# The last FFN with half of its tokens sorted by expert, and their routing done inside the Mamba stage

## The chip, the cores and the metric

The kernel runs on one core of one Trainium2 chip. The metric is device time in microseconds (us). TensorE (PE) multiplies matrices, and its weight loads (PEld) run beside it; VectorE (DVE), ScalarE (ACT) and GpSimd (POOL) do elementwise work; SyncE (SP) issues DMAs. Each engine takes its instructions strictly in the order in which they are written, and the engines wait for each other by semaphores.

## The reference

2048 tokens of 128 channels pass through six stages; the last three are `L1_ffn`, a Mamba layer, and `L1_ffn` again. `L1_ffn` is a mixture of experts with a shared part:

```
xf = layernorm(x).reshape(-1, 128)                       # 2048 tokens
shared = silu(xf @ shared_w1.T) * (xf @ shared_w2.T) @ shared_w3.T      # hidden 512
scores = sigmoid(xf @ router_w.T)                        # 8 experts
_, top_idx = top_k(scores + expert_bias, 2)
gates  = scores * one_hot(top_idx).sum(-2)               # zero for 6 of 8 experts
h1, h2 = split(einsum('td,ehd->teh', xf, w12))           # every token with every expert
routed = einsum('teh,edh->td', silu(h1) * h2 * gates, w3)
x = x + 0.5 * (shared + routed)
```

Only two of the eight experts of a token have a gate that isn't zero.

## The kernel before

The 16 tiles of 128 tokens lie in SBUF for the whole program. An FFN stage takes them in four blocks of 512 tokens (`BLK`), and each block as 12 **units** of 128 hidden channels: 4 shared ones and 8 experts. A unit is two projections (`up`, into the PSUM banks `ps_a` and `ps_b`), Silu on ACT (`gate`), a product on DVE (`gated`), for an expert a product with its gates, broadcast over the partitions, on POOL (`weigh`, L697), a split into a high and a low part on ACT and DVE (`high` L393, `low` L509), and one projection back (`down`, into `ps_acc`). Every projection is three matmuls of 512 columns (`three_pass`, L98 to L100: high times high, low times high, high times low). Experts are dense: each of the 8 is computed for all 512 tokens of a block, and gates of zero cancel 6 of them.

Routing of a block: three matmuls with the router, Tanh, top-8 and indices on DVE (`choose`), gates on POOL (`weights`), a transpose, a store of the gates to DRAM (`gate_rows`) and one broadcast load for each expert (`gate_row`, SP queue, `rows`).

The order is written out by hand. `up` leads by 4 units, `high` and `low` by 2, and every engine runs the same `body(n)`. The stages stand in blocks of their own with a barrier between them. `mamba_phase` runs eight sections (one for each sequence), each of four pieces q = 0 to 3 with `products`, `decay` and `outputs`; four of the sections stand in a hardware loop of two turns, and they also prepare the first two blocks of the following FFN (`turn_head`, `high_head`, `normal_head`: layernorm, transpose, split). The rest of the last sequence (`tail.*`: `to_tokens`, `turn_y`, `project_out`) lies in the beginning of the last FFN. In the first stage the SP queue also loads the weights of all later stages, between the gate rows (`loads`; `load_rest` at L2532 issues after the rows of block 1).

## Time and profile before

| | before |
|---|---|
| median of 3 runs (lowest to highest) | 723.2 us (720.96 to 723.59) |
| profiled execution: its own time | 724.5 us |
| profiled execution: span from first to last instruction | 722.5 us |
| mean granted TensorE clock | 0.987 |
| PE / DVE / ACT / POOL busy | 94% / 79% / 58% / 45% |
| Mamba ends, last FFN begins, last matmul of it begins | 603.35, 604.61, 717.35 us |

A busy PE isn't a PE at its peak: matmuls overlap by their modelled ends, so the distance between two starts, not the duration, is what one costs. The distance of starts within one kind of matmul is read off the timeline.

### The profile page before, as it was taken

The page shows a single profiled execution, that of the slowest core. Times are in us where ns is not written, and L with a number is a line of the kernel's source. Part 1 is how long each engine was busy: PE and PEld are TensorE (multiplying, and loading weights), DVE is VectorE, ACT ScalarE, POOL GpSimd, SP SyncE. Part 2 cuts the span into 40 slices and gives each one's busy share as a digit, 9 for nine tenths or more (in the row PEclk, how much of TensorE's full clock was granted, in tenths as well). Part 3 has the DMA queues.
Part 4 walks back from the last instruction along what each step waited for, and adds up shares of the span by engine and source line. Part 5 has one row for each costly group of instructions (what it writes and reads, how often), then busy time and mean ns, then how long its engine had stood idle before and what let it go on. Part 6 is the DMA issues. An engine that isn't in the chain of part 4 may idle for free. (4 is left out here: it accounts for less than half of the span.)

```text
span 722.5 us, 12386 instructions
## 1 busy us (share of the span) xinstructions
PE 677.4 (94%) x4100; PEld 506.3 (70%) x4100; DVE 569.2 (79%) x1308; ACT 419.3 (58%) x757; POOL 324.5 (45%) x404
## 2 busy tenths in 40 slices
PE   7899998797899999999999878999999998999997
PEld 5667774643457777777778676777777775777785
DVE  5789978989978888988989855666766676879774
ACT  4557686885245555556656647555565555455553
POOL 2568884101227766465658461220413200555463
PEclk9999999999999999999999989999999999999999
DMA  6625430000013232222213100000000000323131
GB/s 168 200 89 187 137 110 1 0 1 0 1 52 125 70 108 90 88 59 81 96 59 90 29 1 1 2 2 2 1 2 0 0 1 2 117 74 118 56 122 44
DMA packets 34329, 43.16 MB, mean 60 GB/s; under 512 B 5216, under 2 KB 17504, under 8 KB 34272
## 3 DMA queue, kind: packets, MB, share of 16 engines
q1 hardware_dynamic: 34272, 42.46, 19.1%
q8 instruction: 29, 0.48, 0.3%
q14 instruction: 28, 0.23, 0.1%
HBM read 41.13 MB, written 1.31 MB: 59 GB/s over the span
## 5 line engine op out<-in xcount | busy, mean ns | idle before, releaser
L697 POOL TENSOR_TENSOR p_prod<-p_p,p_gate_row 128x512 f32<-128x512 f32 x128 | 203.5, 1602 | 108.7 <-DVE p_p L504 62.4
L384 ACT ACTIVATE p_sil<-p_ps_a 128x512 f32<-128x512 f32 x176 | 105.3, 598 | 131.1 <-PE p_ps_a L100 126.8
L509 DVE TENSOR_TENSOR p_hlo<-p_prod,p_hhi 128x512 fp32r<-128x512 f32 x176 | 149.6, 851 | 0.3 <-ACT p_hhi L393 0.2
L504 DVE TENSOR_TENSOR p_p<-p_sil,p_ps_b 128x512 f32<-128x512 f32 x128 | 87.1, 681 | 54.3 <-ACT p_sil L384 37.3
L393 ACT CAST p_hhi<-p_prod 128x512 fp32r<-128x512 f32 x176 | 108.1, 615 | 24.9 <-POOL p_prod L697 24.9
L98 PE MATMUL p_ps_a<-xt_hi,w_uphi 128*128 128x512 f32 x176 | 74.2, 422 | 0.0
L98 PE MATMUL p_ps_acc<-p_hhi,w_downhi 128*128 128x512 f32 x176 | 71.1, 404 | 1.2 <-DVE p_hlo L509 1.0
L98 PE MATMUL p_ps_b<-xt_hi,w_uphi 128*128 128x512 f32 x176 | 71.2, 404 | 0.1
L100 PE MATMUL p_ps_a<-xt_hi,w_uplo 128*128 128x512 f32 x176 | 70.1, 398 | 0.0
L99 PE MATMUL p_ps_a<-xt_lo,w_uphi 128*128 128x512 f32 x176 | 70.1, 398 | 0.0
L100 PE MATMUL p_ps_b<-xt_hi,w_uplo 128*128 128x512 f32 x176 | 69.8, 396 | 0.0
L99 PE MATMUL p_ps_acc<-p_hlo,w_downhi 128*128 128x512 f32 x176 | 69.5, 395 | 0.0
L99 PE MATMUL p_ps_b<-xt_lo,w_uphi 128*128 128x512 f32 x176 | 69.5, 395 | 0.0
L100 PE MATMUL p_ps_acc<-p_hhi,w_downlo 128*128 128x512 f32 x176 | 69.3, 394 | 0.0
L2185 DVE TENSOR_TENSOR mb_sm<-mb_sm,mb_c 128x512 f32<-128x512 f32 x64 | 43.8, 688 | 27.1 <-ACT mb_off L2069 21.1
L1910 PE MATMUL mb_c<-mb_bc 64*128 64x128 f32 (+1 forms) x512 | 58.9, 349 | 1.4 <-ACT mb_bc L2047 1.4
L2047 ACT COPY mb_bc<-mb_c 128x1024 f32<-128x1024 f32 x32 | 32.3, 1012 | 43.8 <-PE mb_c L100 43.8
L1910 PEld LDWEIGHTS mb_c<-mb_bc 64*128 64x128 f32 x512 | 38.9, 186 | 20.9 <-issue 16.0
L2192 DVE SCALAR_TENSOR_TENSOR mb_sm<-mb_d,mb_later 128x512 f32<-128x512 f32 x64 | 41.1, 684 | 15.0 <-PE mb_d L1885 14.8
L2066 ACT ACTIVATE mb_sm<-mb_sm 128x512 f32<-128x512 f32 x64 | 40.5, 632 | 16.9 <-DVE mb_sm L2192 15.9
L2332 POOL TENSOR_TENSOR w_downhi<-mb_widehi,mb_own 128x512 fp32r<-128x512 f32 x8 | 8.3, 1041 | 84.6 <-DVE norm_moments L2211 46.8
L98 PEld LDWEIGHTS p_ps_b<-xt_hi,w_uphi 128*128 128x128 f32 x176 | 33.3, 189 | 11.8 <-DVE p_p L504 2.8
(355 smaller groups left out, 1432.1 us busy)
## 6 DMA issues: line engine op xcount, KB each, us to landing
p_gate_row<-gate_rows SPq DMA_DIRECT2D x128, 256.0 KB, 3.3
w_rawbuf<-in_L_ffn_fc_w_dram SPq DMA_DIRECT2D x3, 512.0 KB, 7.0
w_rawbuf<-in_L_ffn_w_dram SPq DMA_DIRECT2D x3, 512.0 KB, 6.5
out_dram<-x SPq DMA_DIRECT2D x4, 256.0 KB, 3.5
w_rawbuf<-in_L_ffn_shared_w_dram SPq DMA_DIRECT2D x3, 256.0 KB, 5.8
x<-in_L_attn_x_dram SPq DMA_DIRECT2D x2, 256.0 KB, 3.9
x<-in_L_attn_x_dram SPq DMA_DIRECT2D x1, 512.0 KB, 9.2
mb_xraw<-in_L_attn_W_B_dram SPq DMA_DIRECT2D x1, 512.0 KB, 5.0
```

The lines of the kernel that those rows point to most:

```text
L98: pe.matmul(out, weights[0], moving[0], start=start, stop=False)
L99: pe.matmul(out, weights[0], moving[1], start=False, stop=False)
L100: return pe.matmul(out, weights[1], moving[0], start=False, stop=stop)
L384: nc.scalar.activation(sil[:, u % 2], ps_a[:, u % 2], ACT.Silu).then_inc(c["sil"].sem, 1)
L393: nc.scalar.copy(hhi[:, u % R], prod[:, u % R]).then_inc(c["hhi"].sem, 1)
L504: nc.vector.tensor_tensor(dst, sil[:, u % 2], ps_b[:, u % 2], ALU.mult).then_inc(c["p1"].sem, 1)
L509: nc.vector.tensor_tensor(hlo[:, u % R], prod[:, u % R], hhi[:, u % R].bitcast(F32), ALU.subtract).then_inc(c["hlo"].sem, 1)
L697: G.tensor_tensor(prod[:, u % R], p1[:, u % 2], gate_row[:, e % ROWS], ALU.mult).then_inc(c["prod"].sem, 1)
L1910: last = pe.matmul(half(q, t, more)[:, k, 0:SEQ - t * P], bc[h][state, r, j, bass.ts(t, P)], bc[h][state, 2 + r, j, t * P:SEQ], start=True ...
L2066: A(sm[q % 2][t][:], sm[q % 2][t][:], ACT.Exp).then_inc(c["m_E"].sem, 1)
L2185: V.tensor_tensor(sm[q % 2][t][:], sm[q % 2][t][:], half(q, t, more)[:, :, 0:P], ALU.mult).then_inc(c["m_read"].sem, 1)
L2192: V.scalar_tensor_tensor(out=sm[q % 2][t][:], in0=ps_d[t][:], scalar=0.0, in1=later[:].unsqueeze(1).broadcast_to([P, 4, P]), op0=ALU.min, ...
```

## The change

Blocks 0 and 1 of the last FFN (8 tiles, 1024 tokens) keep their 4 shared units; their experts are computed on sorted tokens. Blocks 2 and 3 stay as they are.

- **In Mamba.** The layernormed rows of blocks 0 and 1 stay in `xraw`. `TokenSort.logits` (12 small matmuls for each block), `bend` (Tanh) and `choose` route them in the two loop sections with a `head`; in the last section `rank` (9 matmuls with triangular matrices) and `places` (nine small DVE operations) work out, for each token and each of its two experts, a row of a sorted list in which each expert begins at a multiple of 128. POOL then scatters rows by indirect DMA into `sorted_rows` in DRAM: 4 tiles, two DMAs each, at the end of Mamba, 4 more at the beginning of the FFN. The hardware loops are written out. `outputs(h, m, 0)` stands ahead of `to_tokens` there, and PE waits for the Tanh (`gth`) or for `z_slot` in between, since the logits and ranks lie in `to_tokens`' bank.
- **In the last FFN** (`sparse_stream`, new). `SLOT_TILES` = 23 tiles of 128 sorted rows in six groups (5 of 4, one of 3) follow the four shared units of block 0. PE reads the expert of each tile into a register (`z_owners`, 23 loads spread over units 0 to 3); each tile is transposed, multiplied with the weights of its own expert with the tokens as the stationary side (`three_pass_turned`: 3 matmuls of 256 columns up, 3 of 128 down), stored to DRAM, and gathered by 16 indirect DMAs on POOL. ACT multiplies with the gates (`z_weigh`), POOL adds (`z_add`). The gates of block 2 are applied by DVE, those of block 3 by POOL; there are 8 buffers for gate rows, not 4.
- **In the first stage.** `load_rest` first fills `sorted_rows` with zeros (23 tiles, 1.5 MB).

```diff
+def three_pass_turned(pe, out, tokens, weights):
+    pe.matmul(out, tokens[0], weights[0], start=True, stop=False)
+    pe.matmul(out, tokens[0], weights[1], start=False, stop=False)
+    return pe.matmul(out, tokens[1], weights[0], start=False, stop=True)
...
+    def logits(self, pe, b, xt, router, bank):
+        pe.wait_ge(c["xlo"].sem, c["xlo"].at(b + 1))
+        for j in range(BT):
+            some = bass.ts(b * BT + j, P)
+            last = three_pass(pe, self.logits_of(bank)[:, j], [q[:, some] for q in xt], [q[:] for q in router], True, True)
+        last.then_inc(c["z_lg"].sem, 1)
...
+    def scatter(self, j):
+        for k in range(2):
+            self.nc.gpsimd.indirect_dma_start(self.rows_dram[:, :], bass.IndirectOffsetOnAxis(ap=self.place[:, k, j:j + 1], axis=0),
+                                              self.xn[:, j], None).then_inc(self.c["z_scat"].sem, 16)
...
+            def z_owners(g):
+                for q in range(g * SLOT_TILES // CUT, (g + 1) * SLOT_TILES // CUT):
+                    owner[q] = pe.value_load(sort.owner[0:1, q:q + 1], min_val=0, max_val=(EXPERTS - 1) * P)
...
+            def z_up(s):
+                pe.wait_ge(c["z_xlo"].sem, c["z_xlo"].at(s + 1))
+                for t in range(sizes(s)):
+                    some = bass.ds(owner[s * BT + t] * 2 + S * 2 * P, 2 * P)
+                    last = three_pass_turned(pe, raised(s)[:, t].rearrange("p a c -> p (a c)"),
+                                             [q[s % 2][:, bass.ts(t, P)] for q in (z_xhi, z_xlo)], [q[:, some] for q in up_flat])
...
+            for g in range(CUT):
+                step(g)
+            z_turn_x(1)
+            for s in range(GROUPS):
+                z_up(s)
+                if s:
+                    z_turn_h(s - 1)
+                if s >= 2:
+                    z_down(s - 2)
+                if s + 2 < GROUPS:
+                    z_turn_x(s + 2)
+                if s + 2 == GROUPS:
+                    turn_gates(2)
+            step(CUT)
+            z_turn_h(GROUPS - 1)
+            z_down(GROUPS - 2)
+            step(CUT + 1)
+            z_down(GROUPS - 1)
...
+            scale(2)
+            for j in range(SCATTERED, HALF):
+                sort.scatter(j)
+            scale(3)
+            weights(2)
+            for h in range(2):
+                kept = c[f"z_kept{h}"]
+                pool.wait_ge(kept.sem, kept.at(16 * (GROUPS // 2)))
+            for j in range(HALF):
+                sort.gather(j, z_back)
+                if j == 4:
+                    weights(3)
+            for b in range(2):
+                z_add(b)
...
-            with pe.Fori(0, 2) as i:
+            for i in range(2):
                 section(1, i * 2 + 3)
                 section(0, i * 2 + 4, head=i)
...
         def load_rest(sp):
 
+            sp.dma_start(rows_dram.rearrange("(t p) c -> p t c", p=P), kept["xraw"][:, 0:1].broadcast_to(
+                [P, SLOT_TILES, P])).then_inc(counts["z_blank"].sem, 16)
             w1_set.load(sp, slice(4, None))
             rw_set.load(sp, slice(0, None))
```

**SP in the first stage, between the gate rows of block 1 and of block 2.** Before:

```order
L786 DMA p_gate_row<-gate_rows 128x512 [waits s_prod] x7
L71 DMA w_rawbuf<-in_L_ffn_w_dram 128x4x256
L71 DMA w_rawbuf<-in_L_ffn_w_dram 128x8x128
L71 DMA rw_tm<-in_L_attn_W_tm_dram 128x384
L71 DMA rw_cm<-in_L_attn_W_cm_dram 128x512
L71 DMA rw_cp<-in_L_attn_W_cp_dram 128x4x128
```

The same place now:

```order
L794 DMA p_gate_row<-gate_rows 128x512 [waits s_prod] x7
L3378 DMA sorted_rows<-mb_xraw 128x23x128
L71 DMA w_rawbuf<-in_L_ffn_w_dram 128x4x256
L71 DMA w_rawbuf<-in_L_ffn_w_dram 128x8x128
L71 DMA rw_tm<-in_L_attn_W_tm_dram 128x384
L71 DMA rw_cm<-in_L_attn_W_cm_dram 128x512
L71 DMA rw_cp<-in_L_attn_W_cp_dram 128x4x128
L784 DMA gate_rows<-p_gates_t 32x128 [waits s_gts]
```

The fill of `sorted_rows` goes out ahead of the weight loads and of block 2's gates.

**PE in Mamba's last section, from the end of piece 0's products** (`mb_y` is the bank of `to_tokens`, `z_both` the choices as ones and zeros, `mb_le` and `mb_gt` the triangular matrices). Before, where the third row from below is the first of `to_tokens`:

```order
L1885 MATMUL mb_d<-w_downhi,w_downlo 128x512 [waits r_zf2]
L1885 MATMUL mb_d<-w_downlo 128x512 [waits r_zf2]
L1910 MATMUL mb_c<-mb_bc 128x256 [waits r_tr2]
L1910 MATMUL mb_c<-mb_bc 128x256 x3
L1743 MATMUL mb_y<-ident,mb_yt 128x128 [waits r_c3,r_vv,r_rs2]
L1743 MATMUL mb_y<-ident,mb_yt 128x128 x2
L1933 MATMUL mb_pyt<-mb_sm,mb_xp 32x128 [waits r_tr2,r_rr,r_vv,r_kx]
```

Now, from the ranks on:

```order
L933 MATMUL mb_y<-z_both,mb_le 128x72 [waits z_both,r_c3]
L935 MATMUL mb_y<-z_both,mb_gt 128x64
L935 MATMUL mb_y<-z_both,mb_gt 128x56
L935 MATMUL mb_y<-z_both,mb_gt 128x48
L935 MATMUL mb_y<-z_both,mb_gt 128x40
L935 MATMUL mb_y<-z_both,mb_gt 128x32
L935 MATMUL mb_y<-z_both,mb_gt 128x24
L935 MATMUL mb_y<-z_both,mb_gt 128x16
L935 MATMUL mb_y<-z_both,mb_gt 128x8
L2704 MATMUL mb_d<-w_downhi,w_downlo 128x512 [waits r_zf2]
L2704 MATMUL mb_d<-w_downlo 128x512 [waits r_zf2]
L2729 MATMUL mb_c<-mb_bc 128x256 [waits r_tr2]
```

Nine matmuls are new, and the waits on `z_both` ahead of them and on `z_slot` ahead of `to_tokens` are new.

**PE after the four shared units of block 0 in the last FFN.** Before, an expert's unit stands there, of which this is the second half:

```order
L98 MATMUL p_ps_b<-xt_hi,w_uphi 128x512 [waits s_p1]
L99 MATMUL p_ps_b<-xt_lo,w_uphi 128x512
L100 MATMUL p_ps_b<-xt_hi,w_uplo 128x512
L98 MATMUL p_ps_acc<-p_hhi,w_downhi 128x512 [waits s_hlo]
L99 MATMUL p_ps_acc<-p_hlo,w_downhi 128x512
L100 MATMUL p_ps_acc<-p_hhi,w_downlo 128x512
```

Now groups of sorted tiles; these are the rows from the transposes between two groups on, with the first two tiles of a group (the names `w_uphi` and `w_uplo` stand for the tokens' parts too, which lie in spent weight buffers):

```order
L1193 MATMUL p_ps_o<-ident,mb_zs 128x128 [waits r_c3,r_r]
L1193 MATMUL p_ps_o<-ident,mb_zs 128x128 x3
L1170 MATMUL p_ps_t<-ident,p_z_rows 128x128 [waits r_zf,r_mom]
L1170 MATMUL p_ps_t<-ident,p_z_rows 128x128 x3
L105 ISA [waits r_zf,r_r]
L105 MATMUL p_ps_a<-w_uphi 128x256
L106 REGISTER_ALU
L106 MATMUL p_ps_a<-w_uplo,w_uphi 128x256
L107 MATMUL p_ps_a<-w_uphi,w_uplo 128x256
L105 ISA
L105 MATMUL p_ps_a<-w_uphi 128x256
L106 REGISTER_ALU
```

512-column matmuls give way to 256- and 128-column ones with register instructions between them.

## Rows read from the trace of the kernel before

**Rows 1.** The page: busy time of the engines, and PE's slices.
```profile
PE 677.4 (94%) x4100; PEld 506.3 (70%) x4100; DVE 569.2 (79%) x1308; ACT 419.3 (58%) x757; POOL 324.5 (45%) x404
PE   7899998797899999999999878999999998999997
```

**Rows 2.** A stretch of 10 us: busy PE, PEld, DVE, ACT, POOL, PEclk, DMA.
```profile
600.00:610.00 10.00, 8.13 (x75) 5.78 (x68) 3.78 (x17) 5.34 (x11) 0.00 (x0) 0.83 0.00 0
```

**Rows 3.** Timeline of PE, two units apart and a `turn_out`: start us, duration us.
```profile
691.00 0.39 PE L98 MATMUL p_ps_a<-xt_hi,w_uphi 128*128 128x512 f32 x1
693.09 0.39 PE L98 MATMUL p_ps_a<-xt_hi,w_uphi 128*128 128x512 f32 x1
698.68 0.60 PE L316 MATMUL p_ps_o<-ident,p_acc_s 128*128 128x128 f32 x4
699.03 0.48 PE L98 MATMUL p_ps_acc<-p_hhi,w_downhi 128*128 128x512 f32 x1
```

**Rows 4.** Timeline of PE at the last FFN's beginning.
```profile
604.61 0.59 PE L98 MATMUL p_ps_l<-xt_hi,w_routerhi 128*8 128x512 f32 x1 [0.85 <-PEq L1804]
605.84 0.63 PE L98 MATMUL p_ps_a<-xt_hi,w_uphi 128*128 128x512 f32 x1
615.46 0.33 PE L98 MATMUL p_ps_o<-w_uphi,mb_yThi 128*128 128x128 f32 x1 [0.77 <-DVE mb_yTlo L1778]
615.62 0.27 PE L99 MATMUL p_ps_o<-w_uplo,mb_yThi 128*128 128x128 f32 x1
616.07 0.28 PE L100 MATMUL p_ps_o<-w_uphi,mb_yTlo 128*128 128x128 f32 x1
616.18 0.45 PE L98 MATMUL p_ps_a<-xt_hi,w_uphi 128*128 128x512 f32 x1
```

**Rows 5.** Timeline of PE in Mamba: 256-column matmuls outside and inside the loop.
```profile
491.43 0.39 PE L98 MATMUL mb_c<-xt_hi,w_uphi 128*128 128x256 f32 x1
491.65 0.28 PE L99 MATMUL mb_c<-xt_lo,w_uphi 128*128 128x256 f32 x1
...
558.80 0.38 PE L98 MATMUL mb_c<-xt_hi,w_uphi 128*128 x1
559.02 0.28 PE L99 MATMUL mb_c<-xt_lo,w_uphi 128*128 x1
560.23 0.28 PE L100 MATMUL mb_c<-xt_hi,w_uplo 128*128 x1
```

**Rows 6.** Timeline of DVE in Mamba, and in the FFN (`choose`, first and last operation).
```profile
558.06 0.69 DVE L2185 TENSOR_TENSOR mb_sm<-mb_sm,mb_c 128x512 f32<-128x512 f32 x1 [0.57 <-ACT mb_off L2069]
608.81 0.19 DVE L546 SCALAR_TENSOR_TENSOR p_score<-p_th,minus_half 128x32 f32<-128x32 f32 x1 [5.06 <-ACT p_th L409]
610.35 0.22 DVE L562 TENSOR_TENSOR p_hot<-iota,p_topi 128x64 f32<-128x64 f32 x1
```

**Rows 7.** Timeline of the SP queue in the first stage: start, us of issuing.
```profile
55.39 0.98 SPq L71 DMA_DIRECT2D w_rawbuf<-in_L_ffn_w_dram  x2
60.25 0.32 SPq L776 DMA_DIRECT2D gate_rows<-p_gates_t  x1
64.73 14.07 SPq L786 DMA_DIRECT2D p_gate_row<-gate_rows  x8
```

**Rows 8.** Timeline of POOL there.
```profile
70.49 1.63 POOL L697 TENSOR_TENSOR p_prod<-p_p,p_gate_row 128x512 f32<-128x512 f32 x1 [0.17 <-issue]
```

**Rows 9.** DVE's `low` (ns min/median/max), ACT's `high`, a POOL power, a store's landing.
```profile
L509 DVE TENSOR_TENSOR p_hlo<-p_prod,p_hhi x176: 657/685/2302, 19.7 to 715.8; 128x512 fp32r<-128x512 f32 x176
L393 ACT CAST p_hhi<-p_prod 128x512 fp32r<-128x512 f32 x176 | 108.1, 615 | 24.9 <-POOL p_prod L697 24.9
615.24 1.04 POOL L703 TENSOR_TENSOR norm_rstd<-norm_veps,minus_half 128x4 f32<-128x4 f32 x1
out_dram<-x SPq DMA_DIRECT2D x4, 256.0 KB, 3.5
```

**Rows 10.** Timeline of PE: the last matmul of the last unit.
```profile
717.35 0.40 PE L100 MATMUL p_ps_acc<-p_hhi,w_downlo 128*128 128x512 f32 x1
```

## What was predicted, before the changed kernel had run

> **What bounds the kernel now.** I read the page first, then the stretches of 10 us, then the timeline of PE. PE is busy for 94% of the span, and its slices are full in the FFN stages and in Mamba [rows 1]; the last FFN is an unbroken row of 512-column matmuls. The timeline gives their price: one unit of nine starts 2.09 us after the other (691.00 to 693.09), 0.232 us for a matmul [rows 3]. The only larger loss near the change is the border of Mamba and FFN: PE waits 0.85 us for its own sequencer, and the stretch from 600 to 610 has a mean granted clock of 0.83; at the 1.2 GHz level the three router matmuls take 1.23 us (604.61 to 605.84) instead of 0.70 [rows 2, 4]. So the change pays by the PE work that it removes, and loses what it adds to PE or makes PE wait for.
>
> **PE's work, removed and added.** The sum is made against the profiled span, 722.5 us; its own run took 724.5, the median 723.2, and I carry the difference over to the median.
>
> - Blocks 0 and 1 lose 8 expert units each: 16 x 2.09 = 33.4 us less [rows 3].
> - Ahead of the first `up` of the steady order (616.18 in rows 4) two routers go (1.23 + 0.70), one turn of logits (0.35, priced as four transposes) and one of gates (0.1): 2.4 less. A transpose of four tiles comes in (0.35 [rows 3]), and DVE now measures and normalises block 2 ahead of the tail's products, for which I charge 1.1 us of waiting in `turn_y` and `turn_x`. Net 1.0 less. Later another turn of logits and of gates goes: 0.5 less.
> - The sorted tiles. The nearest rows for 256 columns are Mamba's: 0.12 us each (559.02 to 560.23, ten steps [rows 5]); for 128 columns with new weights 0.112 (615.62 to 616.07, four steps [rows 4]); four transposes take 0.35, so 0.088 each [rows 3]. One tile is 3 x 0.12 + 3 x 0.112 + 2 x 0.088 = 0.87 us, 23 tiles 20.1 us more. This is the point of the change: half-empty tiles included, 23 tiles do the work of 64 (16 units of four tiles).
> - In Mamba: 2 x 12 matmuls of logits and 9 of ranks. They load 128 x 128 weights for few columns; between nothing and the 0.112 of rows 4, I take 0.11 for each, since the weight load stays: 3.6 us more.
> - From 616.18 to 717.58 [rows 4, 10] PE has 101.4 us, of which units are 48 x 2.09 less the four leading `up` at 1.39 (94.8) and routers, transposes and gates 4.6; some 2.0 us are small waits. A third of the units goes: 0.7 less.
>
> Sum without new waits: -33.4 - 1.0 - 0.5 + 20.1 + 3.6 - 0.7 = -11.9 us.
>
> **New waits.** None of these stands in the trace of before, so each has two ends.
>
> - *Filling the groups.* `z_turn_x(1)` shares the bank with `z_turn_x(0)` and waits for ACT's copy (0.62) and DVE's low part (0.66) of it [rows 9], with the hops between them 1.7 us, and nothing stands on PE between the two. After the last group `up` waits 0.6 us for Silu and product. Inside the groups the same chain hides behind 3.3 us of PE work for each group. 2.3 us (1 to 4).
> - *The 23 register loads.* PE's sequencer reads the experts one by one, five or six behind each of four `down`, with the three matmuls of `down` (0.7 us) queued ahead as cover. Behind them stand the next `up`, the router and at last the transposes of the first group. Ends: nothing, and the 0.85 us which PE's sequencer took at the border of the blocks [rows 4]. I take 0.2, nearer to the low end, since a load does less than such a border: 23 x 0.2 - 4 x 0.7 = 1.8 us (0 to 16.8).
> - *Register instructions between matmuls*, one or two for each of 46 products. In the loop of Mamba one stands between the two matmuls at 558.80 and 559.02, which are 0.22 apart; outside the loop, without it, the same two are 0.22 apart too (491.43 and 491.65) [rows 5]. So nothing (up to 0.1 each, 4.6).
> - *Mamba.* `choose` occupies DVE for 1.8 us (608.81 to 610.57 [rows 6]) and now lies in two loop sections, with a sum behind it. The product at 558.06 ends 0.1 us before the piece that PE starts at 558.80 [rows 5, 6], so DVE's lateness passes to PE; DVE's idle time around it (0.57 at that row) takes most of it. In the last section PE waits for `z_slot`, five dependent DVE operations of 0.2 us, with 2 us of its own work in between. I take 2.0 us for all (0 to 8).
> - *The first stage.* The 1.5 MB of zeros go out at 55.4 us ahead of 1.7 MB of weights. Already now the store of block 2's gates, issued at 60.25, holds the first row back until 64.73 [rows 7]: the weights took some 9 us, so the zeros take 6 to 8. The first row is used at 70.49 [rows 8], 2.5 us after it lands. POOL starts some 4 to 5 us late; the lead of two units (4.2 us) covers PE once, but POOL has little idle time there to catch up before it makes block 3's gates. 1.5 us (0 to 5).
> - *POOL's indirect DMAs*, 16 scatters and 16 gathers. Between the 0.32 us that SP takes to issue one [rows 7] and the 1.63 us of POOL's longest product [rows 8]; I take the 1.04 of its power [rows 9]. Then they are hidden: eight scatters fit in the 9 us between `z_place` (about 595 us) and the end of Mamba; the other eight, the last's landing and the load of the first rows (3.5 us each [rows 9]) end 18.5 us into the FFN, PE asks for them at about 20.1; gathers keep ahead of ACT's `z_weigh`, and `weights(3)`, behind ten of them, ahead of `turn_gates(3)`, up to 1.26 us each.
> - *DVE in block 2* has three operations of about 0.6 us in a unit of 2.09; POOL doesn't work on products then, and `low` without it takes its shortest, 0.66, and not up to 2.30 [rows 9]. Nothing.
>
> Waits: 2.3 + 1.8 + 2.0 + 1.5 = 7.6. Balance: -11.9 + 7.6 = -4.3 us, a span of 718.2, a median of **718.9 us**.
>
> Two rules weigh on this. The rows show no register load at all. The Trainium skill (DMA: Bandwidth & Descriptors, Latency and other measured facts) gives a `tensor_load` a floor of about 600 ns. By it the loads would cost 23 x 0.6 - 2.8 = 11.0 us instead of 1.8, and the median would be 728.1; no run here shows it. Of indirect DMAs the rows show none either. The same page (Anatomy of one DMA, SWDGE path) puts a fixed cost of some 2.0 us on each DMA from GpSimd and calls most of it the receipt of the write, which would overlap with the next; by that the scatters land earlier than I assume and the sum stays.
>
> **Rivals.**
>
> *B, the waits hide.* The register loads overlap, DVE's slack takes `choose`, the zeros pass. Then only PE's work counts, with the filling of the groups at its low end: -11.9 + 1 = -10.9, 712.3 us. For it speaks that PE was fed without a gap through all of Mamba [rows 1]; against it, how thin the slack at 558 us is [rows 6].
>
> *C, GpSimd's DMAs set the pace (slower).* At 1.63 us each the eight scatters take 13 us, hold back the barrier behind Mamba by 4, the first rows come 3.1 us late (3.2 + 13.0 + 7.0 against 20.1), and ten gathers hold `turn_gates(3)` back by 3.7: 10.8 us more, 729.7. It is slower than before from about 1.4 us each. For it: POOL is the slowest engine wherever it appears; against it, that a DMA moves nothing through POOL itself.
>
> *D, the register loads block PE (slower).* From 0.39 us each they eat the whole gain; at the middle of the upper half, 0.62, they cost 11.5 us instead of 1.8: 728.6. For it: they can't be skipped, and PE is the bound; against it, that the first transposes of sorted rows would have waited for their rows anyhow.
>
> *E, no change.* Mamba and the first stage cost 4 us more than I take (DVE's chain passes to PE in each of three sections, POOL's lateness in blocks 2 and 3): 722.9.
>
> **How the numbers follow.** My forecast gets 0.40, B 0.17, C 0.15, D 0.13, E 0.15. A measurement tells a difference of about 0.5% (3.6 us) from no change. The forecast stands at -0.6%, so of its 0.40 I count 0.28 as faster and 0.12 as the same; B is faster; of C 0.11 slower and 0.04 the same; of D 0.10 and 0.03; of E 0.04 slower and 0.11 the same. Faster 0.45, same 0.30, slower 0.25. The range reaches from just below B, 710, to C and D, 730; the forecast alone has 714 to 723.
>
> **What would show it.** Right: 32 units of 2.09 us; six groups of some 3.5 us (23 tiles of 0.87); 24 logits at about 0.11 in two Mamba sections; one wait of 1.7 us between the first two row transposes. Register loads: the gap on PE behind each of four `down`; above 0.7 us D grows. C would show as POOL DMAs longer than 1.3 us, a late barrier, and waits of PE for the rows or for the gates. The first stage: PE's gaps between 70 and 100 us, or none. The prediction is wrong if the sorted groups run at more than 4.5 us each, or if Mamba grows by more than 10 us.

## The result: slower by 2.9%

The changed kernel took 744.38 us in the median of 4 runs (736.88 to 747.43), the kernel before 723.39 on the same chip (720.96 to 723.99): a ratio of 1.029, 95% interval 1.026 to 1.032. Forecast were 718.9 us and a range that ended at 730. The profiled execution is the slowest of the four: it took 747.43 us with a span of 745.7, where the kernel before had 724.5 and 722.5. The page of the changed kernel, its busy lines and the slices of PE and of the clock:

```profile
PE 678.1 (91%) x4157; PEld 508.8 (68%) x4157; DVE 561.6 (75%) x1319; ACT 417.3 (56%) x761; POOL 320.8 (43%) x418
...
PE   7899988797999999999999689999999959699697
...
PEclk8999999999999999999999999999999977899899
```

PE is busy for the same total as before, over a span 23 us longer [rows 1]; its lost time and its low clock stand in the last quarter. The stretches there (columns as in rows 2):

```profile
600.00:610.00 10.00, 4.48 (x51) 2.79 (x50) 3.04 (x6) 2.11 (x5) 6.49 (x7) 0.84 0.15 52
610.00:620.00 10.00, 7.05 (x66) 5.35 (x67) 6.43 (x17) 3.59 (x7) 0.00 (x0) 0.50 0.01 2
640.00:650.00 10.00, 6.82 (x33) 5.99 (x32) 4.12 (x11) 3.37 (x6) 0.51 (x2) 0.72 0.19 53
700.00:710.00 10.00, 5.68 (x14) 3.79 (x15) 4.13 (x6) 4.57 (x12) 4.82 (x6) 0.66 0.12 34
```

Where one stretch of the kernel before had a clock of 0.83 [rows 2], here 610 to 620 is wholly at the 1.2 GHz level (0.50), and 640 to 650 and 700 to 710 partly. Each time PE had idled before: between 600 and 610 it is busy for 4.48 us. The timeline of PE (start, duration, and in brackets the idle time ahead and what ended it):

```profile
603.67 1.14 PE L2729 MATMUL mb_c<-mb_bc 64*128 64x256 f32 x8
612.03 0.69 PE L2568 MATMUL mb_y<-ident,mb_ytok 128*128 128x128 f32 x2 [7.22 <-DVE mb_ytok L2591]
...
619.14 0.76 PE L98 MATMUL p_ps_a<-xt_hi,w_uphi 128*128 128x512 f32 x1 [0.92 <-PEq L2622]
...
645.51 1.08 PE L1170 MATMUL p_ps_t<-ident,p_z_rows 128*128 128x128 f32 x4 [1.49 <-DVE w_uplo L1472]
...
660.90 0.55 PE L1170 MATMUL p_ps_t<-ident,p_z_rows 128*128 128x128 f32 x3 [1.25 <-DMA p_z_rows<-sorted_rows]
...
705.73 0.80 PE L98 MATMUL p_ps_b<-xt_hi,w_uphi 128*128 128x512 f32 x1 [2.28 <-DVE p_p L1403]
```

In the kernel before, the wait for the same tile is short:

```profile
599.18 0.44 PE L1750 MATMUL mb_y<-ident,mb_ytok 128*128 128x128 f32 x2 [0.52 <-DVE mb_ytok L1773]
```

The FFN begins at 619.14 and not at 604.61 [rows 4]: 14.5 us, of which 6.1 had gathered in Mamba (the same piece `mb_c` x8 starts at 603.67 instead of 597.53), 6.7 are the wait at 612.03 beyond the 0.52 of before, and 1.7 are left for the time behind it, at the slower clock. From there to the end of the span the changed kernel takes 126.6 us and the one before 117.9, although 16 units are gone; the forecast had 11.4 less. PE's wait at 612.03 is for DVE, and DVE itself stood still:

```profile
602.93 0.69 DVE L3014 TENSOR_TENSOR mb_sm<-mb_sm,mb_c 128x512 f32<-128x512 f32 x1 [0.67 <-ACT mb_off L2896]
609.90 0.69 DVE L3014 TENSOR_TENSOR mb_sm<-mb_sm,mb_c 128x512 f32<-128x512 f32 x1 [6.29 <-remote]
```

```profile
598.22 1.25 POOL L982 DMA_INDIRECT sorted_rows<-mb_xraw,z_place  x1 [25.31 <-DVE z_place L959]
599.76 0.96 POOL L982 DMA_INDIRECT sorted_rows<-mb_xraw,z_place  x1 [0.30 <-issue]
...
607.36 0.96 POOL L982 DMA_INDIRECT sorted_rows<-mb_xraw,z_place  x1 [0.30 <-issue]
```

Eight in a row, 0.96 us each and 0.30 to the next, so one every 1.26 us. In the gathers (684.28 to 705.1) the pattern returns, on ACT:

```profile
693.56 0.60 ACT L1270 ACTIVATE p_sil<-p_ps_a 128x512 f32<-128x512 f32 x1 [1.92 <-remote]
...
701.39 0.60 ACT L1270 ACTIVATE p_sil<-p_ps_a 128x512 f32<-128x512 f32 x1 [6.13 <-remote]
...
707.13 0.60 ACT L1270 ACTIVATE p_sil<-p_ps_a 128x512 f32<-128x512 f32 x1 [4.04 <-remote]
```

Here too it is PE's updates that come late: those for the pieces of `p_ps_a` that ended at 694.11 and 696.21 are recorded at 701.37 and 707.11, and ACT starts 0.02 us behind each. So PE was 7.3 and 10.9 us done before ACT heard of it.

And one wait has a plain reason: ACT's copy of the last group's results waits for a store that SP has behind block 2's gate rows.

```profile
680.94 0.48 ACT L1325 COPY p_z_out<-p_ps_l 128x384 f32<-128x384 f32 x1 [6.22 <-DMA sorted_results<-p_z_out]
```

### The profile page after: what moved, and what is told of

Same layout as the page of the kernel before. It is cut to its first block and busy times, and to the rows that moved or that the text cites. A ratio compares the mean times of both kernels' runs of the same rounds, so it can differ in the third digit from the quotient of the medians.

```text
span 745.7 us, 12381 instructions
## 1 busy us (share of the span) xinstructions
PE 678.1 (91%) x4157; PEld 508.8 (68%) x4157; DVE 561.6 (75%) x1319; ACT 417.3 (56%) x761; POOL 320.8 (43%) x418
## 3 DMA queue, kind: packets, MB, share of 16 engines
q0 software_dynamic: 1024, 2.10, 0.9%
## 5 line engine op out<-in xcount | busy, mean ns | idle before, releaser
L704 POOL TENSOR_TENSOR p_prod<-p_p,p_gate_row 128x512 f32<-128x512 f32 x96 | 150.8, 1583 | 76.4 <-DVE p_p L511 35.5
L391 ACT ACTIVATE p_sil<-p_ps_a 128x512 f32<-128x512 f32 x128 | 76.5, 597 | 87.6 <-PE p_ps_a L100 85.6
L516 DVE TENSOR_TENSOR p_hlo<-p_prod,p_hhi 128x512 fp32r<-128x512 f32 x128 | 109.6, 857 | 0.3 <-ACT p_hhi L400 0.2
L511 DVE TENSOR_TENSOR p_p<-p_sil,p_ps_b 128x512 f32<-128x512 f32 x96 | 65.3, 680 | 38.6 <-ACT p_sil L391 22.9
L400 ACT CAST p_hhi<-p_prod 128x512 fp32r<-128x512 f32 x128 | 78.7, 615 | 21.4 <-POOL p_prod L704 21.4
L98 PE MATMUL p_ps_b<-xt_hi,w_uphi 128*128 128x512 f32 x160 | 65.0, 406 | 3.4 <-DVE p_p L1403 3.3
L99 PE MATMUL p_ps_b<-xt_lo,w_uphi 128*128 128x512 f32 x160 | 63.8, 399 | 0.0
L99 PE MATMUL p_ps_acc<-p_hlo,w_downhi 128*128 128x512 f32 x160 | 63.4, 396 | 0.0
L100 PE MATMUL p_ps_acc<-p_hhi,w_downlo 128*128 128x512 f32 x160 | 63.2, 395 | 0.0
L3021 DVE SCALAR_TENSOR_TENSOR mb_sm<-mb_d,mb_later 128x512 f32<-128x512 f32 x64 | 41.2, 685 | 14.5 <-PE mb_d L2704 12.6
L98 PE MATMUL mb_c<-xt_hi,w_uphi 128*128 128x256 f32 x128 | 38.7, 303 | 3.3 <-DVE mb_sm L3014 1.3
```

The costliest lines, as they stand in the source:

```text
L98: pe.matmul(out, weights[0], moving[0], start=start, stop=False)
L99: pe.matmul(out, weights[0], moving[1], start=False, stop=False)
L100: return pe.matmul(out, weights[1], moving[0], start=False, stop=stop)
L391: nc.scalar.activation(sil[:, u % 2], ps_a[:, u % 2], ACT.Silu).then_inc(c["sil"].sem, 1)
L400: nc.scalar.copy(hhi[:, u % R], prod[:, u % R]).then_inc(c["hhi"].sem, 1)
L511: nc.vector.tensor_tensor(dst, sil[:, u % 2], ps_b[:, u % 2], ALU.mult).then_inc(c["p1"].sem, 1)
```

## The experiments

Theory T1: runs of indirect DMAs on GpSimd hold up engines whose waits are met by the records, and the clock falls behind the gaps. Rivals: T2, the changed Mamba stage itself; T3, a busy GpSimd, whatever it does; T4, the sorted path's own waits (register loads, the order on SyncE). All were timed against the kernel before on the same chip (722.0 to 722.7 us in each set).

| kernel | us | ratio to before, 95% |
|---|---|---|
| b_ind8 | 727.15 | 1.007 (1.005 to 1.010) |
| b_plain8 | 722.49 | 1.000 (0.999 to 1.002) |
| b_pool8 | 722.00 | 1.000 (0.999 to 1.002) |
| b_gap8 | 721.32 | 0.998 (0.997 to 1.000) |
| b_rows16 | 731.61 | 1.012 (1.010 to 1.015) |
| b_g128 | 725.68 | 1.004 (1.003 to 1.006) |
| b_g4 | 724.68 | 1.003 (1.002 to 1.005) |
| a_sp | 724.02 | 1.002 (1.000 to 1.003) |
| a_sp_fixed | 716.57 | 0.992 (0.990 to 0.995) |
| a_sp_keep | 721.95 | 1.000 (0.999 to 1.002) |
| a_gap | 732.80 | 1.015 (1.012 to 1.017) |
| a_gap_keep | 733.93 | 1.017 (1.014 to 1.020) |
| a_early | 733.54 | 1.016 (1.014 to 1.019) |
| a_spread | 734.62 | 1.017 (1.014 to 1.021) |
| a_late0 | 727.67 | 1.008 (1.006 to 1.009) |
| a_late | 729.42 | 1.010 (1.008 to 1.012) |

Where a kernel is said below to lie so much under the changed one, medians of two separate sets are compared, and the changed kernel's own executions lie up to 10.6 us apart. So such a difference is rougher than the ratios. Against the kernel before on its own chip the changed kernel is 21.0 us slower, `a_gap` 10.4, `a_late0` 5.3 and `a_sp` 2.0.

### Eight DMAs in the kernel before

`b_ind8` adds this to POOL at the end of Mamba:

```diff
+            pool.wait_ge(c["m_Y"].sem, c["m_Y"].at((BATCH - 1) * 4 + 1))
+            for j in range(8):
+                nc.gpsimd.indirect_dma_start(consts["d_rows"][:, :], bass.IndirectOffsetOnAxis(
+                    ap=consts["d_at"][:, j:j + 1], axis=0), consts["ident"][:], None).then_inc(consts["d_done"], 16)
```

> The kernel before, with nothing of the sorting in it but eight indirect DMAs of 128 rows that GpSimd issues one after the other at the end of Mamba, where the changed kernel has its first eight; they write to memory that nobody reads, and nothing waits for them. Theory T1 (a run of indirect DMAs on GpSimd holds up engines whose own waits are met): VectorE shows one idle stretch of 4 to 7 us near 595 to 605 us of the span, TensorE's granted clock falls behind it, and the time is 6 to 14 us above the kernel before (730 to 737 us). Rival T2 (the stall belongs to the changed Mamba stage: its unrolled loop, its ranks or its wait for places): no stall, and the time is that of the kernel before within 1 us, 723 us.

`b_plain8` has `nc.gpsimd.dma_start(consts["d_rows"][bass.ts(j, P)], consts["ident"][:])` in its place, `b_pool8` twelve products.

> The kernel before with eight plain DMAs of 128 rows of 512 bytes, issued by GpSimd at the same place. If what holds the others up is the work of issuing DMAs on GpSimd, plain ones do it as well: 6 to 14 us above the kernel before where each takes about as long to issue as an indirect one (1.26 us). If it is the indirection (reading 128 places and building 128 descriptors), the time is that of the kernel before within 1 us, 723 us.

> The kernel before with twelve ordinary GpSimd products of 128x256 (about 0.8 us each, some 10 us in a row) at the same place, and no DMA. T1: nothing happens, 723 us within 1 us. Rival T3 (a GpSimd that is busy without a break takes the SBUF from VectorE, whatever it does): VectorE's operations in that stretch grow or wait, and the time is 3 us or more above the kernel before.

Measured: 5.1 us more, nothing, nothing. The 5.1 us are less than the 6 to 14 that I had expected, and VectorE's idle stretch is 3.67 us (to 597.32), not 4 to 7. T2 and T3 fall as causes of the stall: it comes into a kernel that sorts nothing, and neither a busy GpSimd nor eight plain DMAs of the same size bring it. `b_ind8`, timelines of POOL and PE:

```profile
589.99 1.24 POOL L2387 DMA_INDIRECT extra_rows<-ident,d_at  x1 [21.90 <-PE mb_pyt L1934]
...
599.09 0.96 POOL L2387 DMA_INDIRECT extra_rows<-ident,d_at  x1 [0.30 <-issue]
```
```profile
599.47 0.69 PE L1751 MATMUL mb_y<-ident,mb_ytok 128*128 128x128 f32 x2 [4.29 <-DVE mb_ytok L1774]
```

In `b_plain8` the eight take 4.5 us together, not 10; a row of plain ones as long as the burst was not tried:

```profile
589.53 4.52 POOL L2387 DMA_DIRECT2D extra_rows<-ident  x8 [21.93 <-PE mb_pyt L1934]
```

### Which property of the burst

`b_gap8` puts two products of 128x256 behind each indirect DMA and begins a sequence earlier; `b_rows16` takes `d_at[0:16]` and `ident[0:16]`; `b_g128` and `b_g4` stand at the first place with one product of 128x128 or of 128x4 between.

> The kernel before with the same eight indirect DMAs, but two GpSimd products of 128x256 between each and the next (a pitch of about 2.9 us in place of 1.26) and begun one sequence earlier, so that they lie between about 573 and 596 us, a whole sequence of Mamba. If only an unbroken run of them holds the others up, the time is that of the kernel before within 1 us (722 us) and no idle stretch of VectorE over 1.5 us stands in there. If each indirect DMA has its price wherever it stands, the time is 4 us or more above the kernel before, as with the eight in a row (727 us).

> The kernel before with eight indirect DMAs in a row at the first place, of 16 rows each instead of 128. If the stall goes with the rows, for which GpSimd has to write descriptors, each takes well under 0.9 us to issue and the time is that of the kernel before within 1 us (722 us). If it goes with the instruction, 727 us again and 0.96 us each.

> The kernel before with the eight indirect DMAs of 128 rows at the first place (from about 590 us), and one GpSimd product of 128x128 between each and the next: a pitch of about 1.9 us. The pitch of 2.6 us that cost nothing also lay a sequence earlier, so the place could have saved it. If the gap is what matters: 721 to 723 us, and TensorE's semaphore updates arrive in their usual order. If the place does (TensorE's updates are held in that part of the program whenever indirect DMAs are under way): 727 us or more, as with the eight in a row.

> The same with a product of 128x4 between each and the next, a pitch of about 1.6 us. If any other GpSimd instruction between two indirect DMAs is enough, 721 to 723 us; if it takes idle time in the DMA path of which 0.3 us more is too little, 725 to 731 us.

I missed `b_rows16`: with an eighth of the rows an indirect DMA takes 0.85 us, hardly less, and the kernel is 9.4 us slower than the one before, more than with all rows. Its timelines of POOL, DVE and PE:

```profile
591.14 1.10 POOL L2387 DMA_INDIRECT extra_rows<-ident,d_at  x1 [21.87 <-PE mb_pyt L1934]
...
599.46 0.85 POOL L2387 DMA_INDIRECT extra_rows<-ident,d_at  x1 [0.30 <-issue]
```
```profile
594.12 0.69 DVE L2186 TENSOR_TENSOR mb_sm<-mb_sm,mb_c 128x512 f32<-128x512 f32 x1 [0.67 <-ACT mb_off L2070]
602.61 0.69 DVE L2186 TENSOR_TENSOR mb_sm<-mb_sm,mb_c 128x512 f32<-128x512 f32 x1 [7.79 <-remote]
```
```profile
595.20 1.14 PE L1911 MATMUL mb_c<-mb_bc 64*128 64x256 f32 x8
604.73 0.69 PE L1751 MATMUL mb_y<-ident,mb_ytok 128*128 128x128 f32 x2 [8.40 <-DVE mb_ytok L1774]
```

PE goes on here while DVE stands: at 594.53, 594.87 and 595.20 it starts new pieces. The semaphore events of the trace name what is late. PE's update for the piece that ended at 594.6 is recorded at 602.51; its next three, for pieces up to 596.3, at 602.55, 602.58 and 602.67; one due at 594.0 at 599.65. Of ACT's and DVE's own updates the trace lacks a few in there; those that it has come in time. So the products are done, but the news of them is late: here by up to 7.9 us, most of it until 2.2 us after the last of the eight has ended. In `b_ind8` the same updates come at 597.23 to 597.30 instead of from 593.5 on, while the burst still runs. In `a_sp` (below) and in the kernel before, none of PE's updates behind 600 us comes more than 0.05 us after its piece. And behind 560 us, idle time of DVE or ACT that "remote" ends stands in only three of the eighteen traces, those of the changed kernel, `b_ind8` and `b_rows16`: the three with indirect DMAs in an unbroken row.

The wait follows the pitch, the time from the start of one indirect DMA to the start of the next. Timelines of POOL and PE in `b_gap8`, of PE in `b_g128` and in `b_g4`:

```profile
573.74 1.01 POOL L2387 DMA_INDIRECT extra_rows<-ident,d_at  x1 [0.28 <-POOL d_sink L2391]
...
576.37 1.00 POOL L2387 DMA_INDIRECT extra_rows<-ident,d_at  x1 [0.28 <-POOL d_sink L2391]
```
```profile
595.37 0.44 PE L1751 MATMUL mb_y<-ident,mb_ytok 128*128 128x128 f32 x2 [0.52 <-DVE mb_ytok L1774]
```
```profile
596.64 0.44 PE L1751 MATMUL mb_y<-ident,mb_ytok 128*128 128x128 f32 x2 [0.63 <-DVE mb_ytok L1774]
...
606.06 0.58 PE L98 MATMUL p_ps_l<-xt_hi,w_routerhi 128*8 128x512 f32 x1 [4.85 <-PEq L1805]
```
```profile
597.20 0.44 PE L1751 MATMUL mb_y<-ident,mb_ytok 128*128 128x128 f32 x2 [1.65 <-DVE mb_ytok L1774]
```

PE's wait for `mb_ytok` is 8.40 us at a pitch of 1.15 us, 4.29 at 1.26, 1.65 at 1.50, 0.63 at 1.72 and 0.52 at 2.63 (that burst ended at 590.6, and PE has no wait of 0.3 us or more in it). The kernel before has 0.52 us there as well. The first two of these differ in rows and in pitch at once; the others have 128 rows each. `b_g4`, which I had expected to be either level or at 725 us and more, lies 2.3 us above the kernel before: its wait is 1.1 us longer, and the clock from 600 to 610 is 0.61 instead of 0.83. The 3.3 us of `b_g128`, again more than I had expected, are another matter: its last DMA ends at 604.2, and the border between the stages waits for POOL, 4.85 us instead of 0.85. That the place in the program matters is excluded by it too, since it stood where `b_ind8` did.

### The changed kernel without its indirect DMAs

In `a_sp` SyncE's queue takes plain DMAs of the same 64 KB, so rows go to fixed places and the result isn't sorted. GpSimd is thereby free of all 32, and block 3's gates no longer stand behind ten of them; the work of the other engines stays.

```diff
-            self.nc.gpsimd.indirect_dma_start(self.rows_dram[:, :], bass.IndirectOffsetOnAxis(ap=self.place[:, k, j:j + 1], axis=0),
-                                              self.xn[:, j], None)
+            self.nc.sync.dma_start(self.rows_dram[bass.ts(2 * j + k, P)], self.xn[:, j])
```

> The changed kernel with its 32 indirect DMAs replaced by plain ones of the same 64 KB on SyncE's queue; rows go to fixed places and not to the sorted ones, everything else (ranks, owners, register loads, groups, gates) stays. T1: the stall of 7.2 us at the end of Mamba, the gaps at 632 us and at 690 to 711 us and most of the clock's falls are gone, and the time is 15 to 25 us under the changed kernel: 720 to 729 us. Rival T4 (the sorted path's own waits, register loads and order of DMAs cost the time): at most 4 us are gained, 740 us or more.

724.02 us: 20.4 under the changed kernel (19.0 when each is set against the kernel before on its own chip), as T1 had it; T4 had at most 4. That is the price of the indirect DMAs in every way: late updates, the clock behind them, and GpSimd's time. This is the main finding; but even so the kernel is only level with the one before. `a_sp_fixed` adds this, and with it gives up the choice of the expert:

```diff
-                    owner[q] = pe.value_load(sort.owner[0:1, q:q + 1], min_val=0, max_val=(EXPERTS - 1) * P)
+                    owner[q] = q // 3 * P
```

> The changed kernel with plain DMAs of SyncE (724.0 us) and, besides, with the group of weights of each sorted tile fixed in the program: none of the 23 register loads on TensorE. It leaves out the choice of the expert for a tile. Rival T4 (the register loads cost about 5 us, of which the prediction had 1.8): the gaps of 1.1, 1.4 and 1.7 us behind the four first downs are gone, 719 to 721 us. If they are covered by waits that stay: 723 to 724 us.

7.4 us less, and under the 719 to 721 that I had expected: what T4 names costs that much, and is second to the indirect DMAs. Timelines of PE in `a_sp` and in `a_sp_fixed`:

```profile
611.10 0.47 PE L98 MATMUL p_ps_a<-xt_hi,w_uphi 128*128 128x512 f32 x1 [0.92 <-PEq L2623]
...
621.52 0.40 PE L98 MATMUL p_ps_l<-xt_hi,w_routerhi 128*8 128x512 f32 x1 [0.34 <-issue]
...
625.57 0.38 PE L1133 MATMUL p_ps_t<-ident,p_logits_t 8*128 8x8 f32 x4 [1.09 <-issue]
...
629.67 0.50 PE L98 MATMUL p_ps_a<-xt_hi,w_uphi 128*128 128x512 f32 x1 [1.43 <-issue]
...
633.70 0.63 PE L1168 MATMUL p_ps_t<-ident,p_z_rows 128*128 128x128 f32 x4 [1.66 <-issue]
635.81 0.63 PE L1168 MATMUL p_ps_t<-ident,p_z_rows 128*128 128x128 f32 x4 [1.49 <-DVE w_uplo L1470]
```
```profile
609.48 0.77 PE L98 MATMUL p_ps_a<-xt_hi,w_uphi 128*128 128x512 f32 x1 [0.92 <-PEq L2623]
...
630.42 0.63 PE L1168 MATMUL p_ps_t<-ident,p_z_rows 128*128 128x128 f32 x4 [1.82 <-DVE w_uplo L1470]
```

From the first `up` to `z_turn_x(1)` it is 24.7 us with loads and 20.9 without: 3.8. From the second of these marks to `turn_out(0)` (663.58 and 657.17) it is 27.8 and 26.7: at most 1.1 for the register instructions between the sorted products. The rest of the 6.9 us between the spans lies ahead of the FFN (1.6, where the programs are the same and profiles differ by as much) and behind `turn_out(0)` (0.5). What a load takes stands in the trace too (line 1158 of `a_sp`, in ns, on PE's sequencer):

```profile
L1158 PEldq TENSOR_LOAD <-mb_cut x23: 294/301/484, 618.0 to 632.9; - x23
L1158 PEldq FUSED_REGOPS  x23: 146/146/165, 618.6 to 633.3; - x23
L1158 PEldq SEQ_ASSERT  x23: 18/18/28, 618.8 to 633.5; - x23
```

With its register instruction and its assertion, one load starts 0.64 us after the other where they stand in a row, so 23 take 14.7 us. The four gaps of PE (0.34, 1.09, 1.43, 1.66) sum to only 4.5, because the loads run while PE works off what was issued before them, and that covers 10.2 us in all. So a whole unit or more covers each group of loads, and not only the three matmuls of `down`: from 625.57 to 629.67 six loads take 3.8 us, PE works off transposes and nine matmuls in 2.7, and the gap is 1.43.

`a_sp_keep` is `a_sp` (with its register loads) and this:

```diff
-            z_keep(2)
+            for s in range(2, 4):
+                z_keep(s)
             rows(2)
-            for s in range(3, GROUPS):
+            for s in range(4, GROUPS):
                 z_keep(s)
```

> The kernel with plain DMAs and fixed groups, and SyncE stores the fourth group's results ahead of the gate rows of block 2 instead of behind them. ScalarE's wait of 6.0 us for that store is gone. If it cost TensorE what the windows show there (some 1.5 us between 660 and 680), the time is 1 to 2 us under the one with fixed groups alone; if the next wait takes its place, within 0.5 us of it.

The text on record calls it a kernel with fixed groups, which it is not, so it is to be compared with `a_sp`: 2.1 us less, about the size expected.

### Keeping the sorting

`a_gap` is the changed kernel with a product of 128x128 ahead of every indirect DMA (`self.pause()` in `scatter` and `gather`), `a_gap_keep` has the new order on SyncE as well.

> The changed kernel as it is, sorting included, with a GpSimd product of 128x128 ahead of each of the 32 indirect DMAs, which makes the pitch about 1.9 us in place of 1.26. T1 (unbroken runs do the harm): the stalls go, and what is left of the loss is the price of the later ends (the scatters end near 630 us, the gathers near 702): 724 to 728 us, which is 16 to 20 us under the changed kernel although GpSimd does 11 us more work. T4 or a price per indirect DMA: 742 us or more.

> The same, and SyncE stores the fourth group's results ahead of block 2's gate rows, which took 2.1 us off the version with plain DMAs (724.0 to 721.9 us). 1 to 3 us under the one with gaps alone, 722 to 726 us.

`a_gap` is 11.6 us under the changed kernel with more work on POOL, but 5 us over what I expected; `a_gap_keep` is 8 us over. Timeline of PE in `a_gap`:

```profile
605.30 0.44 PE L2579 MATMUL mb_y<-ident,mb_ytok 128*128 128x128 f32 x2 [1.12 <-DVE mb_ytok L2602]
...
690.19 0.40 PE L1155 MATMUL p_ps_t<-ident,p_gates 128*32 128x128 f32 x1 [6.58 <-POOL p_gates L1577]
```

The end of Mamba is sound: 1.12 us in place of 7.22. But block 3's gates (`weights(3)`) stand behind ten gathers on POOL, which now take 20 us. That is 6.6 us. The new order on SyncE brings PE there earlier, and it waits 8.7 us: the two come out alike. `a_early` computes the gates behind six gathers (`if j == 2` for `if j == 4`); `a_spread` places the loads one by one.

> The changed kernel, sorting included, with the gaps between indirect DMAs, the earlier store of the fourth group, and block 3's gates computed by GpSimd after six gathers instead of ten. In the version with gaps TensorE waited 6.6 us for these gates (8.7 us with the earlier store) at 690 us. If that was what the gaps still cost, and the early store gives its 2 us as it did with plain DMAs: 722 to 725 us. If the gathers' own end (702 us) is waited for next: 728 us or more.

> The same with the 23 register loads taken apart: one behind each three products of the units 4 to 7 and of the first four downs, the rest one behind each sorted tile of the first groups, in place of five or six in a row behind each of four downs. With the groups fixed in the program and no load at all the time was 7.4 us less. If a load is covered by the products queued ahead of it: 4 to 7 us under the version above (716 to 720 us, the first under the kernel before). If each load stops TensorE's sequencer until what is queued has ended and then costs its own time: within 1.5 us of it.

Neither moved. ACT in `a_early` weighs gathered rows ahead of the units' own Silu, and waits for them:

```profile
687.09 0.69 ACT L1343 ACTIVATE mb_xraw<-mb_xraw,z_gate 128x128 f32<-128x128 f32 x2 [2.70 <-DMA mb_xraw<-sorted_results,z_place]
...
693.70 0.69 ACT L1343 ACTIVATE mb_xraw<-mb_xraw,z_gate 128x128 f32<-128x128 f32 x2 [4.93 <-DMA mb_xraw<-sorted_results,z_place]
```

These waits sum to 17 us, and so take the place of the one removed. In `a_spread` the loads leave no gaps ahead of the groups, but the wait for the scatters' rows does, and loads between sorted tiles leave 0.21 and 0.28 us (at 644.94 and 645.84):

```profile
634.15 0.66 PE L1187 MATMUL p_ps_t<-ident,p_z_rows 128*128 128x128 f32 x4 [3.98 <-DMA p_z_rows<-sorted_rows]
```

`a_late0` gives `z_weigh` the steps 4, 6, 8, 10, 12, 13, 15 and 17 of block 2 on instead of 2 to 9, lets VectorE weigh half of block 3's units, and puts `z_add(1)` behind POOL's other half; `a_late` has the spread loads too.

> The version with gaps, early store and early gates (733.5 us), and ScalarE's weighing of gathered rows spread over block 2 and the start of block 3 at the gathers' own pace, half of block 3's weighings moved from GpSimd to VectorE, and the second half of the sorted rows added behind GpSimd's weighings. If ScalarE's 17 us of waits for gathered rows were what held TensorE (1.4, 0.6 and 3.3 us of gaps, and the clock at 0.71 behind them): 723 to 727 us. If GpSimd's late end holds block 3 anyway: 731 us or more.

> The same with the register loads taken apart (as in the version that measured 734.6 us). The first sorted rows cannot come before the spaced scatters end (about 627 us, TensorE waited 4.0 us for them), so of the 7.4 us that loads cost with plain DMAs at most 1.2 us can come back before the first group: 0.5 to 3 us under the version above, 721 to 726 us.

727.67 us for `a_late0`: 16.7 under the changed kernel, with the sorting kept, though 0.8% above the kernel before (0.6 to 0.9). It changes three things at once, and no run here takes them apart. The stretch from 690 to 700 in `a_early` and in `a_late0`:

```profile
690.00:700.00 10.00, 6.08 (x16) 4.50 (x16) 4.69 (x8) 4.95 (x12) 8.27 (x12) 0.71 0.58 178
```
```profile
690.00:700.00 10.00, 10.00 (x47) 8.10 (x46) 7.82 (x12) 7.47 (x16) 8.54 (x11) 1.00 0.63 211
```

Loads one by one do not help (1.8 us more, where I had expected 0.5 to 3 less): `a_late` waits 4.5 us for its rows at 632.27. No kernel run here beats the one before and still sorts.

## Why the prediction failed

- **POOL's indirect DMAs: the step that failed.** I took 1.04 us each and "then they are hidden". The pitch of 1.26 was within my ends, and below the 1.4 from which rival C turned the kernel slower. What wasn't in the sum, or in any rival, is that while a run of them lasts PE's semaphore updates come late, by up to 6.7 us in the scatters and 10.9 in the gathers. The sum had nothing for these DMAs; `a_sp` puts the price of all 32 at 19 to 20 us, nearly the whole difference of 21.0 between the changed kernel and the one before. `a_gap`, which keeps all 32 and only spaces them, gives back 11 of these. Part is the clock, how large a part isn't separated: the gap at 612 is followed by a stretch at 0.50. C was right that GpSimd's DMAs make it slower and wrong on how: no late barrier, and no gates late until gaps stretched the gathers.
- **Work of PE.** A unit is 2.1 us as predicted; a group at the 2.4 GHz level takes 3.6 us (652.62 to 656.24) against 3.5. With neither bursts nor loads (`a_sp_fixed`) the FFN takes 106.6 us instead of 117.9, 11.3 less; my terms for it, without loads, make 13.2.
- **Register loads.** Taken at 0.2 us each with 0.7 us of cover for each group of them: 1.8 us. Measured, 0.64 us each and 2.5 of cover, which leaves 4.5 us of gaps, 3.8 net ahead of the groups. Both terms were more than three times too small. They nearly cancelled, and it is luck that the term missed by 2 us and not by ten: the right price with my cover would have made 11.9. Rival D had the price (0.62) and not the cover, so its 11.5 us didn't come. The gaps were where I said. The floor of about 600 ns that the Trainium skill (DMA: Bandwidth & Descriptors, Latency and other measured facts) gives a `tensor_load` agrees with the trace's 0.64 us from one load to the next; the load alone is recorded with 0.30.
- **Register instructions between products.** Taken as nothing (up to 4.6); at most 1.1 us for all, near the low end.
- **Mamba.** 3.6 + 2.0 predicted, 6.1 measured up to the same piece. The nine ranks took 0.12 each; the wait for `z_slot` cost nothing.
- **The first stage.** 1.5 us predicted for the zeros, nothing found: Mamba's first `mb_d` starts at 438.12 us, and at 438.32 in the kernel before.
- **Filling.** `z_turn_x(1)` waited 1.49 us (1.7 predicted). Not foreseen: the last group's rows (1.25 us at 660.90) and ACT's 6.22 us for the store, worth 2.1 by `a_sp_keep`.
- **The signs I named** would have sent a reader to POOL ("POOL DMAs longer than 1.3 us"), and not to where it shows, on PE's consumers. One of them came true by the wrong cause: "if Mamba grows by more than 10 us". The FFN begins 14.5 us later, but 6.7 of these are the wait under the scatters.
- **What is left without the indirect DMAs.** `a_sp` stands 5.1 us over the forecast. Loads and register instructions together cost 7.4 us there where the sum had 1.8, and the store on SyncE 2.1 where it had nothing; against them stand the 1.5 for the zeros, which didn't come. The rest isn't taken apart.

## What to carry to other kernels

Don't issue indirect DMAs from GpSimd in an unbroken row while TensorE's results are waited for: with 0.4 us of other work between them, a pitch of 1.7 us, the late waits were gone here, but then the ends come later, so look at what stands behind them in each queue. An engine's "remote" idle time with its inputs complete by the records asks for a look at what the others issue in that time. And a repair moves nothing while a wait stands behind it: the new order on SyncE and the earlier gates moved nothing, until `a_late0` also took ScalarE's waits for gathers out of the units' way. Last, read the price of a register load off its own records and not off the gaps that it leaves: what was issued ahead hides most of it.

## What the hardware showed that I had not expected

- TensorE's semaphore updates come up to 8 us late in `b_rows16`, and up to 11 in the changed kernel, while GpSimd issues indirect DMAs every 1.15 to 1.26 us. With 16 rows instead of 128 it is worse; the pitch is then shorter too, and whether that is the reason isn't separated. In the bursts the trace also holds only 27 (`b_ind8`) and 32 (`b_rows16`) of the 128 updates of the DMAs themselves, with a pitch of 1.72 us 83, with 2.63 all. What is shared between the two isn't shown by any run here. Nor is it shown whether the recording of the trace, which loses events just there, has a part in it, or whether another engine's updates would be late at a busier place.
- An indirect DMA occupies GpSimd for 0.96 us with 128 rows and 0.85 with 16; a plain one of the same 64 KB takes 0.57. From issue to the first semaphore update it is 2.3 us (589.99 to 592.30).
- A register load holds TensorE's sequencer for 0.64 us in a row of them (0.30 for the load, the rest for what goes with it), while matmuls issued before it run on: of 14.7 us in `a_sp` 4.5 showed as gaps.
